# Quantised rows transposed in bfloat16 instead of float32, in a fused attention and integer-FFN kernel

## The chip, the cores and the metric

The kernel runs on one core of one Trainium2 chip. The metric is the device time of one execution in microseconds (us). A core has five engines that run side by side and wait for each other by semaphores: TensorE (PE in the profile; PEld is its weight load), VectorE (DVE), ScalarE (ACT), GpSimd (POOL) and SyncE (SP, which here only issues DMAs and waits). TensorE reads SBUF and writes PSUM banks; the other engines copy results out of the banks.

## The reference

`x` is (8, 512, 256) in f32. For each of 8 batches it is scaled by a style and normalised, goes through an attention with 16 heads of 16 columns whose projections are demodulated, gets a skip term, and then an FFN quantised to 8 bits whose result is added to `x`:

```python
x = x * s1[:, None, :];  x = (x - mu) * rsqrt(var + EPS_IN)
q = heads(einsum('bsh,oh->bso', x, q_weight) * q_dc);  k = ...;  v = ... * v_dc * s2
out = softmax(q k^T * scale) v
y = (out @ w_weight.T) * w_dc + (v_flat @ u_weight.T) * u_dc
# FFN, 8-bit integers:
lhs_scale = maximum(max(abs(y), axis=2), 1e-12) / 127
q_lhs = clip(round(y / lhs_scale), -127, 127)
q_rhs = clip(round(rhs / rhs_scale), -127, 127)
out = x + (q_lhs @ q_rhs) * lhs_scale * rhs_scale
```

## The kernel before

The program handles one batch per step, t = 0 to 7, in eight slots of a step (`for i in range(SUPER)`). A slot has two rounds of attention: `scores_of` (L1000), ScalarE's exponentials (L524) and `values_of` (L1014), and between them TensorE does "fill" work, listed by `step_fills` and issued by `fill` (L1211): projections for the next batch a = t+1, and the output and the FFN for the batches behind, z = t-1 and y = t-2. The order on each engine is written out by hand; `step_fills` also numbers the uses of a ring of three PSUM banks (`work`), which TensorE claims (`claim`, a wait on `work_freed`) and VectorE frees.

The FFN of batch z, in two halves i of 256 rows each: `output` (L1139) multiplies the attention result by the output weights; `quantise` on VectorE (L741) adds the skip term, takes each row's largest magnitude, forms the scale and its inverse, and makes integers in f32 that have the number MAGIC = 1.5 x 2^23 added, which rounds them; `quantised_transposed` (L1163) transposes them on TensorE by the f32 identity, all through the helper at L977; `integers` (L762) copies them out of the bank and takes MAGIC off again, with a bf16 result (`y_qt`), since whole numbers up to 127 are exact in bf16; `int_product` (L1179) multiplies them by the quantised right side in bf16. In a middle step the two transposes of batch z stand in slot 7 (before `output(z, 1)` and the norms) and slot 8 (behind the values of the next batch, the last work before the flag). The tile `y_q` is a view of the tile `o_t2`; the profile calls both `o_t`.

At the end of a step a flag is computed on VectorE (`bound_flag`, L687): whether the scores of the next batch are small enough to do without a shift by the row maximum. TensorE (`row_maxima`), SyncE (`load_shift`) and VectorE each load it into a register and branch on it; `scores_of` then waits until SyncE has said that the shift is done with.

The last batch has no further attention to hide behind; its two halves go through other banks and ScalarE.

At the start VectorE makes `head_ones` from the identity (L813), clears `q_stack` (L815), copies the transposed conditions (L817) and takes the statistics of the first batch; GpSimd meanwhile fills `k_stack` (L354) and `v_aug` (L357). The root of the variance is GpSimd's (L363), the normalisation VectorE's (L626).

Of the kernel before, what the change touches and what calls it, by code (L numbers as in the profile page):

```python
# [7 lines left out]
BF16 = mybir.dt.bfloat16  # L8
I32 = mybir.dt.int32
ALU = mybir.AluOpType  # L10
# [3 lines left out]
P = 128  # L14
INT8_MAX = 127.0
MAGIC = 1.5 * 2.0 ** 23
# [48 lines left out]
def adaln_ffn_kernel(nc, x, cond, wq, wk, wv, ww, wu, rhs, out):  # L65
    B, S, H = x.shape
    NH, D = 16, H // 16
    KT = S // P
    HC = H // P
# [34 lines left out]
    with ctx:  # L104
        def sb(name, shape, dt=F32):
            return ctx.enter_context(nc.sbuf_tensor(name, shape, dt))

        def sem(name):
            return ctx.enter_context(nc.semaphore(name))

        ident = sb("ident", [P, P])
# [59 lines left out]
        y_q = o_t2[:, :, :, :].rearrange("p i c t -> p (i c t)").rearrange("p (k o) -> p k o", k=KT)  # L171
# [4 lines left out]
        y_inv = sb("y_inv", [P, KT])  # L176
        demod_rows = o_nat[:, :, :].rearrange("p k h -> p (k h)")[0:B, 0:3 * H].rearrange(
            "b (m o) -> b m o", m=3)
        y_qt = sb("y_qt", [P, HC, S], BF16)


        by_two = [o_t2[:, :, :, :].rearrange("p m c t -> p (m c t)").rearrange("p (m c i) -> p m c i", m=2, c=HC),
# [30 lines left out]
        work_ready, work_freed = sem("work_ready"), sem("work_freed")  # L213
# [9 lines left out]
        on_ready, ot_ready, yq_ready, yqt_ready = sem("on_ready"), sem("ot_ready"), sem("yq_ready"), sem("yqt_ready")  # L223
# [359 lines left out]
        def _(dve):  # L583
            chain, taken = Tally(), Tally()

            def link(instruction):

                instruction.then_inc(dve_step, 1)
                chain.count += 1
                dve.wait_ge(dve_step, chain.count)  # L590

            def ready(*key):

                use = USE[key]
                assert use == taken.count, key
                taken.count += 1
                dve.wait_ge(work_ready, use + 1)
                return work[:, use % NW, :]
# [142 lines left out]
            def quantise(z, i):  # L741
                two = slice(2 * i, 2 * i + 2)
                y, scale = y_q[:, two, :], y_scale[:, z % 2, two]
                if z == B - 1:
                    dve.wait_ge(product_t, i + 1)
                    bank = work[:, USE[("y", z, i)] % NW, :]
                else:
                    bank = ready("y", z, i)
                link(nc.vector.tensor_tensor(y, bank.rearrange("p (k o) -> p k o", k=2), skip[:, z % 2, two, :], ALU.add))  # L749
                if z < B - 1:  # L750
                    dve.sem_inc(work_freed, 1)
                link(nc.vector.tensor_reduce(amax[:, two], y, AX.X, ALU.max, apply_absolute_value=True))  # L752
                link(nc.vector.tensor_scalar(scale, amax[:, two], EPS_AMAX, 1.0 / INT8_MAX, ALU.max, ALU.mult))
                link(nc.vector.reciprocal(y_inv[:, two], scale))
                for k in range(2):
                    last = nc.vector.tensor_scalar(y_q[:, 2 * i + k, :], y[:, k, :], y_inv[:, 2 * i + k:2 * i + k + 1],  # L756
                                                   -INT8_MAX, ALU.mult, ALU.max)
                link(last)
                nc.vector.tensor_scalar(y_q[:, two, :], y_q[:, two, :], INT8_MAX, MAGIC, ALU.min, ALU.add
                                        ).then_inc(yq_ready, 1)  # L760

            def integers(z, i):  # L762
                link(nc.vector.tensor_scalar(y_qt[:, :, 2 * i * P:2 * (i + 1) * P],
                                             ready("yqt", z, i).rearrange("p (c t) -> p c t", c=HC), MAGIC, None,
                                             ALU.subtract))
                dve.sem_inc(yqt_ready, 1)
                dve.sem_inc(work_freed, 1)

# [43 lines left out]
            with nc.allow_low_precision("sums of zeros and one 1"):  # L812
                link(nc.vector.tensor_reduce(head_ones[:, 0:HG].rearrange("p (e r) -> p e r", e=2),  # L813
                                             ident[:, :].rearrange("p (e d r) -> p e r d", e=2, d=D), AX.X, ALU.add))
            nc.vector.memset(q_stack[:, 0, :, :].bitcast(F32), 0.0).then_inc(q_cleared[0], 1)  # L815

            link(nc.vector.tensor_copy(cond_t[:, :, :], ready("cond", 0, 0)[:, 0:2 * HC * B].rearrange(  # L817
# [47 lines left out]
            for c in range(HC):  # L865
                bank = ready("xt", 0, c)
# [108 lines left out]
        def _(pe):  # L975
# [3 lines left out]
            def claim(*key):  # L979

                use = USE[key]
                if use >= NW:
                    pe.wait_ge(work_freed, use - NW + 1)
                return work[:, use % NW, :]
# [135 lines left out]
            def transpose_pair(bank, src, i, done):  # L1120

                for c in range(HC):
                    for k in range(2):
                        last = transpose(bank[:, (2 * c + k) * P:(2 * c + k + 1) * P],
                                         src[:, 2 * i + k, c * P:(c + 1) * P])
                last.then_inc(done, 1)
# [36 lines left out]
            def quantised_transposed(z, i):  # L1163
                pe.wait_ge(yq_ready, z * 2 + (i + 1))
                if z == B - 1:
                    transpose_pair(scores[:, 2 + i, :], y_q, i, integers_t)
                else:
                    transpose_pair(claim("yqt", z, i), y_q, i, work_ready)

            def int_product(z, i):  # L1170
                pe.wait_ge(yqt_ready, z * 2 + (i + 1))
# [245 lines left out]
```

## Time and profile before

| | us |
|---|---|
| median of three runs | 459.09 |
| the three runs | 459.18, 459.09, 457.11 |
| the profiled execution | 456.99 |
| its span in the profile | 455.2 |
| TensorE busy | 422.0 (93%) |
| ScalarE busy | 294.4 (65%) |
| VectorE busy | 243.1 (53%) |
| GpSimd busy | 108.2 (24%) |

Busy shares are taken over the whole span. TensorE's products overlap, and their ends in the profile are modelled, so the start-to-start distance of two groups tells what a group costs. "Idle before" in a row is the time in which the engine stood just ahead of that instruction, with the one that released it.

### The profile page before, as it was taken

The numbers are of one execution on the slowest core, as the hardware profiler recorded it, in microseconds if no ns is written. First come the engines' busy times: TensorE is split into PE (matmuls) and PEld (weight loads), VectorE is DVE, ScalarE is ACT, GpSimd is POOL, SyncE is SP. The second block draws the span as 40 slices with busy tenths as digits, with TensorE's granted clock in tenths as the row PEclk, the third lists the DMA queues.
The fourth block names the chain that finished last, engine by engine and source line by source line (L and its number), as shares of the span: only waits on it lengthen the run. The fifth ranks groups of instructions, "written<-read, shape, count | busy, mean of one in ns | idle before, by whom it ended". The sixth has DMA issues, their size and how long they took to land.

```text
span 455.2 us, 7727 instructions
## 1 busy us (share of the span) xinstructions
PE 422.0 (93%) x2684; PEld 233.9 (51%) x2684; DVE 243.1 (53%) x562; ACT 294.4 (65%) x343; POOL 108.2 (24%) x114
## 2 busy tenths in 40 slices
PE   8976499999999999999999999999999999999974
PEld 7744154455554555555545555455545555554444
DVE  6661346454466546745675447654675445436325
ACT  3523278767776686668765786667676776677741
POOL 7292212301111023301250024302340123002111
PEclk9797799999999999999999999999999999999999
DMA  5299239903991189215991299217961299102021
GB/s 174 85 131 155 30 120 137 117 8 111 135 125 55 35 175 147 67 50 149 132 137 54 92 142 139 93 36 151 136 102 55 68 132 159 49 1 94 0 94 46
DMA packets 29470, 44.59 MB, mean 98 GB/s; under 512 B 3896, under 2 KB 15160, under 8 KB 29400
## 3 DMA queue, kind: packets, MB, share of 16 engines
q1 hardware_dynamic: 27184, 38.71, 49.6%
q0 software_dynamic: 1040, 3.70, 2.5%
q10 hardware_dynamic: 1200, 1.59, 2.2%
q8 instruction: 26, 0.43, 0.5%
q14 instruction: 20, 0.16, 0.2%
HBM read 14.57 MB, written 4.25 MB: 41 GB/s over the span
## 4 chain that ended last, share of the span: by engine, by line
PE 81%; DVE 9%; DMA 5%; issue 3%; ACT 2%; DVEq 0%; POOL 0%; POOLq 0%
PE o_acc L1014 23%; PE scores L1000 16%; PE work L1065 10%; PE work L1042 9%; PE work L977 8%; PE work L1139 5%; DMA rows<-rows_dram 3%; PE work L1053 3%; DMA rows_dram<-o_nat 2%; PE work L1179 2%; DVE o_t L756 1%; PE work L1298 1%; DVE amax L752 1%; DVE o_t L749 1%; PE scores L1042 1%
## 5 line engine op out<-in xcount | busy, mean ns | idle before, releaser
L524 ACT ACTIVATE probs<-scores 128x1024 f32<-128x1024 f32 x256 | 247.8, 1024 | 111.2 <-PE scores L1000 111.2
L1014 PE MATMUL o_acc<-probs,v_aug 128*32 128x512 f32 x1024 | 124.4, 602 | 6.8 <-DVE skip L665 6.5
L1000 PE MATMUL scores<-q_stack,k_stack 50*128 50x512 f32 x512 | 96.6, 452 | 9.4 <-DMA k_stack<-parts 4.2
L402 POOL TENSOR_TENSOR squares<-parts 128x512 bf16<-128x512 f32 x32 | 33.5, 1048 | 208.2 <-ACT parts L508 208.2
L1000 PEld LDWEIGHTS scores<-q_stack,k_stack 50*128 50x128 f32 x512 | 39.6, 187 | 82.8 <-ACT probs L524 57.9
L1014 PEld LDWEIGHTS o_acc<-probs,v_aug 128*32 128x32 f32 x1024 | 26.6, 109 | 68.5 <-issue 56.0
L1065 PE MATMUL work<-vs_w,x_t 128*128 128x512 f32 x192 | 53.2, 420 | 0.9 <-DVEq L891 0.9
L1042 PE MATMUL work<-x_t,qk_w 128*128 128x512 f32 x168 | 44.5, 406 | 0.2 <-DVEq L634 0.2
L663 DVE TENSOR_TENSOR v_aug<-work,rows 128x256 f32<-128x256 f32 x32 | 13.6, 424 | 57.8 <-PE work L1065 44.5
L1065 PEld LDWEIGHTS work<-vs_w,x_t 128*128 128x128 f32 x192 | 35.9, 197 | 14.3 <-issue 6.2
L410 POOL TENSOR_TENSOR res<-res,x_res 128x512 f32<-128x512 f32 x15 | 19.1, 1275 | 73.9 <-DVEq L785 73.9
L1042 PEld LDWEIGHTS work<-x_t,qk_w 128*128 128x128 f32 x168 | 30.0, 188 | 7.1 <-issue 0.7
L977 PE MATMUL work<-ident,o_t 128*128 128x128 f32 x180 | 26.5, 276 | 0.0
L1139 PE MATMUL work<-w_demod,o_t 128*128 128x256 f32 x112 | 26.5, 379 | 0.0
L977 PEld LDWEIGHTS work<-ident,o_t 128*128 128x128 f32 x180 | 20.7, 140 | 6.4 <-issue 4.0
L532 ACT ACTIVATE o_t<-o_acc 128x512 f32<-128x512 f32 x32 | 19.2, 599 | 6.1 <-PE o_acc L1014 5.9
L1139 PEld LDWEIGHTS work<-w_demod,o_t 128*128 128x128 f32 x112 | 20.6, 190 | 2.7
L779 DVE SCALAR_TENSOR_TENSOR res<-work,y_scale,rhs_scale_row 128x256 f32<-128x256 f32 x28 | 12.3, 479 | 15.3 <-PE work L1179 15.0
L645 DVE SCALAR_TENSOR_TENSOR parts<-work,cols,parts 128x512 fp32r<-128x512 f32 x14 | 10.5, 750 | 17.7 <-ACT parts L508 17.7
L737 DVE COPY o_t<-work 128x512 f32<-128x512 f32 x14 | 9.7, 692 | 18.6 <-PE work L977 18.2
L626 DVE TENSOR_SCALAR x_sb<-x_sb,mv,rstd 128x256 f32<-128x256 f32 x32 | 11.3, 416 | 11.0 <-issue 11.0
L749 DVE TENSOR_TENSOR o_t<-work,skip 128x512 f32<-128x512 f32 x16 | 11.1, 692 | 11.0 <-PE work L1139 8.5
(149 smaller groups left out, 416.5 us busy)
## 6 DMA issues: line engine op xcount, KB each, us to landing
q_stack<-parts SPq DMA_DIRECT2D x96, 128.0 KB, 6.0
k_stack<-parts SPq DMA_DIRECT2D x88, 128.0 KB, 7.6
x_res<-in_x_dram SPq DMA_DIRECT2D x8, 512.0 KB, 4.3
x_sb<-in_x_dram SPq DMA_DIRECT2D x7, 512.0 KB, 3.6
out_dram<-res POOLq DMA_DIRECT2D x7, 512.0 KB, 6.9
rows<-rows_dram SPq DMA_DIRECT2D x8, 384.0 KB, 3.3
rows<-in_cond_dram SPq DMA_DIRECT2D x8, 128.0 KB, 3.6
k_stack<-parts ACTq DMA_DIRECT2D x8, 128.0 KB, 9.9
```

What stands on the lines that cost most here:

```text
L402: nc.gpsimd.tensor_tensor(squares[:, n, :], parts[:, n, 0, :], parts[:, n, 0, :], ALU.mult).then_inc(squares_ready, 1)
L410: nc.gpsimd.tensor_tensor(res[:, two, :], res[:, two, :], x_res[:, two, :], ALU.add).then_inc(res_added, 1)
L524: nc.scalar.activation(probs[:, r % RING, pair:pair + 2, :], scores[:, pair:pair + 2, :], ACT.Exp).then_inc(exp_done, 1)
L532: nc.scalar.activation(o_t[:, group % G, :], o_acc[:, :], ACT.Copy).then_inc(o_saved, 1)
L749: link(nc.vector.tensor_tensor(y, bank.rearrange("p (k o) -> p k o", k=2), skip[:, z % 2, two, :], ALU.add))
L977: return nc.tensor.transpose(dst, src, ident[0:rows, 0:rows])
L1000: last = nc.tensor.matmul(scores[:, 2 * (u % 2) + e, :], k_stack[top:top + ROWS, t % 2, 2 * g + u % 2, kt * P:(kt + 1) * P], q_stack[top:t ...
L1014: last = nc.tensor.matmul(o_acc[DV * j:DV * (j + 1), :], v_aug[:, kt, 4 * g + j, :], probs[:, r % RING, j, :], start=(kt == 0), stop=(kt = ...
L1042: last = nc.tensor.matmul(bank, lhs, right, start=(n == 0), stop=(n == len(operands) - 1))
L1053: last = nc.tensor.matmul(bank[:, hc * H:(hc + 1) * H], wv_scaled[:, c, hc * P:(hc + 1) * P], wu_t[:, c, :], start=(c == 0), stop=(c == HC ...
L1065: last = nc.tensor.matmul(bank, lhs, right, start=(n == 0), stop=(n == len(operands) - 1))
L1139: last = nc.tensor.matmul(bank[:, k * H:(k + 1) * H], o_t2[:, i, c, k * P:(k + 1) * P], w_demod[:, z % 2, c, :], start=(c == 0), stop=(c = ...
```

## The change

For batches 0 to 6, `quantise` multiplies by the inverse scale and adds MAGIC in the first operation (before: multiply and lower bound), still f32 and in place, and then takes MAGIC off and applies the upper bound 127 in the second, with a bf16 result in a new tile `y_int`. TensorE transposes `y_int` by an ordinary product with a bf16 identity, `ident_b`, in place of the f32 transposes. `integers` applies the lower bound -127 in the copy out of the bank, where it took MAGIC off before. `ident_b` is cast once from the f32 identity, on VectorE at the start, with a wait on its result behind it. The last batch is as before.

```diff
--- before.py
+++ after.py
@@ -177,6 +177,8 @@
         demod_rows = o_nat[:, :, :].rearrange("p k h -> p (k h)")[0:B, 0:3 * H].rearrange(
             "b (m o) -> b m o", m=3)
         y_qt = sb("y_qt", [P, HC, S], BF16)
+        y_int = sb("y_int", [P, KT, H], BF16)
+        ident_b = sb("ident_b", [P, P], BF16)
 
 
         by_two = [o_t2[:, :, :, :].rearrange("p m c t -> p (m c t)").rearrange("p (m c i) -> p m c i", m=2, c=HC),
@@ -752,6 +754,15 @@
                 link(nc.vector.tensor_reduce(amax[:, two], y, AX.X, ALU.max, apply_absolute_value=True))
                 link(nc.vector.tensor_scalar(scale, amax[:, two], EPS_AMAX, 1.0 / INT8_MAX, ALU.max, ALU.mult))
                 link(nc.vector.reciprocal(y_inv[:, two], scale))
+                if z < B - 1:
+                    for k in range(2):
+                        last = nc.vector.tensor_scalar(y_q[:, 2 * i + k, :], y[:, k, :], y_inv[:, 2 * i + k:2 * i + k + 1],
+                                                       MAGIC, ALU.mult, ALU.add)
+                    link(last)
+
+                    nc.vector.tensor_scalar(y_int[:, two, :], y, MAGIC, INT8_MAX, ALU.subtract, ALU.min
+                                            ).then_inc(yq_ready, 1)
+                    return
                 for k in range(2):
                     last = nc.vector.tensor_scalar(y_q[:, 2 * i + k, :], y[:, k, :], y_inv[:, 2 * i + k:2 * i + k + 1],
                                                    -INT8_MAX, ALU.mult, ALU.max)
@@ -761,8 +772,8 @@
 
             def integers(z, i):
                 link(nc.vector.tensor_scalar(y_qt[:, :, 2 * i * P:2 * (i + 1) * P],
-                                             ready("yqt", z, i).rearrange("p (c t) -> p c t", c=HC), MAGIC, None,
-                                             ALU.subtract))
+                                             ready("yqt", z, i).rearrange("p (c t) -> p c t", c=HC), -INT8_MAX, None,
+                                             ALU.max))
                 dve.sem_inc(yqt_ready, 1)
                 dve.sem_inc(work_freed, 1)
 
@@ -812,6 +823,7 @@
             with nc.allow_low_precision("sums of zeros and one 1"):
                 link(nc.vector.tensor_reduce(head_ones[:, 0:HG].rearrange("p (e r) -> p e r", e=2),
                                              ident[:, :].rearrange("p (e d r) -> p e r d", e=2, d=D), AX.X, ALU.add))
+                link(nc.vector.tensor_copy(ident_b[:, :], ident[:, :]))
             nc.vector.memset(q_stack[:, 0, :, :].bitcast(F32), 0.0).then_inc(q_cleared[0], 1)
 
             link(nc.vector.tensor_copy(cond_t[:, :, :], ready("cond", 0, 0)[:, 0:2 * HC * B].rearrange(
@@ -1165,7 +1177,14 @@
                 if z == B - 1:
                     transpose_pair(scores[:, 2 + i, :], y_q, i, integers_t)
                 else:
-                    transpose_pair(claim("yqt", z, i), y_q, i, work_ready)
+
+                    bank = claim("yqt", z, i)
+                    for c in range(HC):
+                        for k in range(2):
+                            last = nc.tensor.matmul(bank[:, (2 * c + k) * P:(2 * c + k + 1) * P],
+                                                    y_int[:, 2 * i + k, c * P:(c + 1) * P], ident_b[:, :],
+                                                    start=True, stop=True)
+                    last.then_inc(work_ready, 1)
 
             def int_product(z, i):
                 pe.wait_ge(yqt_ready, z * 2 + (i + 1))
```

The changed kernel has other line numbers, so rows are matched by operation and names. VectorE at the start of the program, before (L815 clears `q_stack`, L841 scales the first batch by its style):

```order
L810 MEMSET head_ones 128x16
L813 TENSOR_REDUCE head_ones<-ident 128x8
L815 MEMSET q_stack 128x4096
L817 COPY cond_t<-work 128x32
L820 TENSOR_TENSOR cond_sq<-cond_t 128x32
L841 TENSOR_TENSOR x_sb<-x_sb,rows 128x512
```

and of the change:

```order
L821 MEMSET head_ones 128x16
L824 TENSOR_REDUCE head_ones<-ident 128x8
L826 CAST ident_b<-ident 128x128
L827 MEMSET q_stack 128x4096
L829 COPY cond_t<-work 128x32
L832 TENSOR_TENSOR cond_sq<-cond_t 128x32
L853 TENSOR_TENSOR x_sb<-x_sb,rows 128x512
```

The cast of the identity stands between the reduction and the memset; the rest follows in the same order.

TensorE from slot 7 of a middle step to the flag, before (`o_t` in the first row is the quantised tile; L1139 is `output`, L1073 the norms, L1065 the values of the next batch, and the last row of transposes holds both `to_natural` and the quantised rows):

```order
L977 MATMUL work<-ident,o_t 128x128 x4
L1139 MATMUL work<-w_demod,o_t 128x256 x4
L1073 MATMUL work<-squares,head_ones 32x512 x4
L1000 MATMUL scores<-q_stack,k_stack 128x512 x4
L1014 MATMUL o_acc<-probs,v_aug 32x512 x8
L1000 MATMUL scores<-q_stack,k_stack 128x512 x4
L977 MATMUL work<-ident,norm_max 1x128
L1065 MATMUL work<-vs_w,x_t 128x512 x6
L977 MATMUL work<-ident,o_t 128x128 x8
```

and of the change (L1184 is the new product, L1151 the `output` that was L1139):

```order
L1184 MATMUL work<-ident_b,y_int 128x128 x4
L1151 MATMUL work<-w_demod,o_t 128x256 x4
L1085 MATMUL work<-squares,head_ones 32x512 x4
L1012 MATMUL scores<-q_stack,k_stack 128x512 x4
L1026 MATMUL o_acc<-probs,v_aug 32x512 x8
L1012 MATMUL scores<-q_stack,k_stack 128x512 x4
L989 MATMUL work<-ident,norm_max 1x128
L1077 MATMUL work<-vs_w,x_t 128x512 x6
L989 MATMUL work<-ident,o_t 128x128 x4
L1184 MATMUL work<-ident_b,y_int 128x128 x4
```

The two groups of four stand where they stood; only their kind changes.

VectorE in the same slot, `quantise` and the norms behind it, before:

```order
L749 TENSOR_TENSOR o_t<-work,skip 128x512
L752 TENSOR_REDUCE amax<-o_t 128x2
L753 TENSOR_SCALAR y_scale<-amax 128x2
L754 RECIPROCAL y_inv<-y_scale 128x2
L756 TENSOR_SCALAR o_t<-o_t,y_inv 128x256 x2
L759 TENSOR_SCALAR o_t<-o_t 128x512
L673 TENSOR_REDUCE norm_max<-work 128x1
```

and of the change:

```order
L751 TENSOR_TENSOR o_t<-work,skip 128x512
L754 TENSOR_REDUCE amax<-o_t 128x2
L755 TENSOR_SCALAR y_scale<-amax 128x2
L756 RECIPROCAL y_inv<-y_scale 128x2
L759 TENSOR_SCALAR o_t<-o_t,y_inv 128x256 x2
L763 TENSOR_SCALAR y_int<-o_t 128x512
L675 TENSOR_REDUCE norm_max<-work 128x1
```

The number of operations and their shapes stay; the last of `quantise` writes `y_int`.

## Rows read from the trace of the kernel before

**Rows 1.** the page, its busy shares (part 1) and the chain that ended last (part 4).

```profile
PE 422.0 (93%) x2684; PEld 233.9 (51%) x2684; DVE 243.1 (53%) x562; ACT 294.4 (65%) x343; POOL 108.2 (24%) x114
...
PE 81%; DVE 9%; DMA 5%; issue 3%; ACT 2%; DVEq 0%; POOL 0%; POOLq 0%
```

**Rows 2.** timeline: start us, us, engine, operation, [idle before <-releaser]; slot 7 of a middle step.

```profile
232.83 0.66 PE L977 MATMUL work<-ident,o_t 128*128 128x128 f32 x4
...
233.32 1.89 PE L1139 MATMUL work<-w_demod,o_t 128*128 128x256 f32 x8
...
235.25 0.69 DVE L749 TENSOR_TENSOR o_t<-work,skip 128x512 f32<-128x512 f32 x1 [1.04 <-PE work L1139]
...
236.71 1.88 POOL L389 TENSOR_SCALAR wv_scaled<-wv_nat,cols 128x256 f32<-128x256 f32 x2
...
238.31 0.55 DVE L759 TENSOR_SCALAR o_t<-o_t 128x512 f32<-128x512 f32 x1
...
239.51 0.27 PE L977 MATMUL work<-ident,norm_max 128*1 128x128 f32 x1 [0.79 <-DVE norm_max L673]
```

**Rows 3.** timeline of a middle step's end.

```profile
390.58 0.14 DVE L687 TENSOR_SCALAR flag<-bound 1x1 int32<-1x1 f32 x1
...
390.67 1.03 PE L977 MATMUL work<-ident,o_t 128*128 128x128 f32 x8
...
392.46 0.73 PE L1000 MATMUL scores<-q_stack,k_stack 50*128 50x512 f32 x4 [0.76 <-SPq L273]
```

**Rows 4.** timeline: two products of the integers, then transposes.

```profile
226.94 0.61 PE L1179 MATMUL work<-rhs_q,y_qt 128*128 128x256 bf16 x4
...
227.39 0.60 PE L977 MATMUL work<-ident,o_t 128*128 128x128 f32 x4
```

**Rows 5.** timeline of the last step, TensorE.

```profile
419.26 1.09 PE L977 MATMUL work<-ident,o_t 128*128 128x128 f32 x8
...
421.21 0.50 PE L1000 MATMUL scores<-q_stack,k_stack 50*128 50x512 f32 x2 [0.42 <-ACT probs L524]
...
426.03 0.50 PE L1000 MATMUL scores<-q_stack,k_stack 50*128 50x512 f32 x2 [0.34 <-ACT probs L524]
```

**Rows 6.** single lines of VectorE: duration ns min/median/max.

```profile
L763 DVE TENSOR_SCALAR y_qt<-work x14: 683/692/692, 133.7 to 424.9; 128x512 bf16<-128x512 f32 x14
...
L759 DVE TENSOR_SCALAR o_t<-o_t x16: 426/428/554, 127.0 to 447.8; 128x512 f32<-128x512 f32 x16
```

**Rows 7.** the same view, line L621.

```profile
L621 DVE TENSOR_SCALAR var_eps<-mv x7: 170/170/347, 35.5 to 333.5; 128x4 f32<-128x4 f32 x7
```

**Rows 8.** timeline of the program's start, VectorE, GpSimd and TensorE.

```profile
1.78 0.38 DVE L813 TENSOR_REDUCE head_ones<-ident 128x8 bf16<-128x128 f32 x1 [0.90 <-POOL ones L352]
...
2.07 3.51 POOL L354 MEMSET k_stack<- 128x4096 f32 x1
...
3.08 3.47 DVE L815 MEMSET q_stack<- 128x4096 f32 x1 [0.92 <-DVE head_ones L813]
...
6.19 1.83 POOL L357 MEMSET v_aug<- 128x2048 f32 x1
...
10.49 1.05 POOL L363 TENSOR_TENSOR rstd<-var_eps,half 128x4 f32<-128x4 f32 x1 [2.46 <-DVE var_eps L849]
...
12.50 1.37 DVE L626 TENSOR_SCALAR x_sb<-x_sb,mv,rstd 128x256 f32<-128x256 f32 x4
...
18.07 5.47 PE L1042 MATMUL scores<-x_t,qk_w 128*128 128x512 f32 x12
```

**Rows 9.** timeline: a later GpSimd memset and L621 beside it.

```profile
32.28 3.51 POOL L425 MEMSET q_stack<- 128x4096 f32 x1
...
35.47 0.35 DVE L621 TENSOR_SCALAR var_eps<-mv 128x4 f32<-128x4 f32 x1
```

**Rows 10.** the chain in order of time: start us, us, what.

```profile
34.17 14.54 DMA rows<-rows_dram
```

**Rows 11.** a stretch: us, busy (x) of PE, PEld, DVE, ACT, POOL, PEclk, DMA, GB/s.

```profile
16.80:23.60 6.80, 6.80 (x22) 5.35 (x22) 2.66 (x5) 3.30 (x7) 3.25 (x8) 0.50 0.31 104
```

## The prediction

> **What bounds the kernel now.** I read the page's busy shares first, then the chain of waits, then the timeline of one middle step, of the last step and of the first 50 us, and last the groups of instructions by shape. TensorE is busy for 93% of the span and carries 81% of the chain that ended last; VectorE has 9% of it [rows 1]. A middle step (one batch of attention, in eight slots) is a TensorE stream with two places where it stands. In the seventh slot TensorE waits for a VectorE chain: the product L1139 ends, VectorE adds, reduces and quantises (L749 to L759), then takes the largest norms (L673), and only then can TensorE transpose the norms: 0.79 us idle at 239.51 [rows 2]. At the step's end TensorE waits until the flag has been read: in the 390 us step the eight transposes start at 390.67 and end at 391.70, the scores start at 392.46, released by SyncE (L273), while the flag was written at 390.58 + 0.14 = 390.72 [rows 3]. The scores come 1.74 us behind the flag, and the transposes end 0.76 us earlier than that.
>
> **TensorE: what is removed.** Each batch but the last has two groups of four f32 transposes of the quantised rows; the change makes each a group of four bf16 products, 14 groups in all. A group costs from 232.83 to the start of L1139 at 233.32, 0.49 us [rows 2]. No row shows a bf16 product with 128 columns. The nearest is L1179, bf16 with 256 columns: four take from 226.94 to 227.39, 0.11 us each [rows 4]. Halving the columns gives at best 0.055 us each; if the weight loads set the pace it stays 0.11. The last one still has to cover the load of f32 weights for L1139, for which I leave 0.11. I take 3 x 0.055 + 0.11 = 0.28 us for a group, a gain of 0.21 us; the ends are a gain of 0.05 (pace 0.11 throughout, 0.44) and of 0.27 (0.22 in all). A group slower than 0.49 I exclude: L1179 moves twice the columns in 0.45.
> The Trainium skill, "TensorE: Matmul & The Clock Gate", section "Back-to-back issue gap", gives about 81 ns for each pair of a weight load and a 128-column product in a stream; by it a group would be 0.32 us or a little more and the gain up to 0.17, an estimate from that page, which no row here shows.
>
> **Which groups lie on the path.** The first group of a batch (slot 7) stands before L1139, whose end releases VectorE's add after an idle VectorE [rows 2], and everything up to the norms, the values, the flag and the next scores hangs on that. So its 0.21 us passes through, in six middle steps: 6 x 0.21 = 1.26 us. The second group (slot 8) is the later half of the eight transposes at 390.67. It ends before the flag has been read, so a faster group only lengthens the idle time: gain 0 in six steps, as long as the scores wait for the flag [rows 3]. Of the last two groups, in the last step, the first is in the eight at 419.26; the scores behind it wait for ScalarE's exponentials (0.42 us idle at 421.21), and the second group stands before such a wait too (0.34 us idle at 426.03) [rows 5]. Gain 0. TensorE in all: -1.3 us, not 14 x 0.21 = 2.9.
>
> **VectorE in the steps.** The two operations with the scale (L756) keep form and shape. The third, L759, 128x512 f32 in place in 426 to 554 ns, now writes bf16. The one bf16 write of that size that VectorE does in the steps takes 692 ns, but it reads from a bank (L763); L759 reads from SBUF [rows 6]. I take no change; the upper end is 692 ns. On the path lies only the one in slot 7, which took 0.55 us beside GpSimd's L389 [rows 2]: at 0.69 it would cost 6 x 0.14 = 0.8 us. The lower end, were half the bytes quicker, is some 0.1 us each, 0.6 in all. The copy out of the bank (L763) keeps its size and its one operation: 0.
>
> **VectorE at the start: what is added.** One cast of the identity, 128x128 f32 to bf16, goes between the reduction L813 and the memset of q_stack L815, with a wait behind it. Alone it is cheap: between L621's 170 ns (4 elements [rows 7]) and L759's 426 (512), so about 0.23 us, plus 0.15 for the wait. Behind it on VectorE are the memset, the copy of the conditions (L817), the modulation and statistics of the first batch; GpSimd's root (L363) waits for them, and VectorE's L626 for the root. The root is done at 10.49 + 1.05 = 11.54 and L626 starts at 12.50, so there is 0.96 us of cover [rows 8]. Alone the cast is hidden.
> But GpSimd starts its memset of k_stack at 2.07 and holds it until 5.58 [rows 8], while L813 ends at 2.16. The trace has one like pair: L621, VectorE's tensor-scalar in SBUF, began at 35.47 while GpSimd's memset L425 ran to 35.79. It took 347 ns against 170 in its other runs, and ended at 35.82, just behind the memset [rows 7, 9]. Against it: L759 beside GpSimd's tensor-scalar L389 lost 0.12 us, though L389 stood on GpSimd from 236.71 to 238.59 [rows 2]. So the bounds are 0 (hidden) and a cast held until 5.58, or even until the second memset ends at 6.19 + 1.83 = 8.02 [rows 8]. By the row nearest in kind, L621, I take the first memset. The cast then ends near 5.73, 3.57 us after L813. The q_stack memset ended 4.39 us after L813 (6.55 against 2.16), so it ends near 10.1, and L817, the statistics and the root come 3.6 us later. After the cover of 0.96, L626 is 2.6 to 2.7 us late. On it hang the transposes, the first projections (18.07), the store of the row scales and the load of rows, which lands at 34.17 + 14.54 = 48.7 and for which the first values wait [rows 10]. Nothing on that way is idle for another reason, so I take +2.7. The granted clock from 16.8 to 23.6 is 0.50, the 1.2 GHz level [rows 11]; how much of the projections falls into such a stretch can move this by about 0.5 either way.
> The Trainium skill, "SBUF — State Buffer", section "Who interferes with whom", says that GpSimd and a VectorE copy, cast or tensor-scalar between SBUF tiles that uses both port pairs exclude each other for a whole instruction. By that rule the cast waits for the memset; L621's 347 ns agrees with it, L759 beside L389 only in part; a cast held to 5.58 is what the sum already has.
>
> **The sum.** The profiled execution took 456.99 us, span 455.2 plus 1.8 around it. -1.3 (TensorE) + 0 (quantising) + 2.7 (start) = +1.4: 458.4 for such an execution. The three runs have a median of 459.09 and the profiled one lies below all of them; the four average 458.1. I apply the +1.4 to that mean, 459.5.
>
> **Rivals.**
> 1. The cast is not held: it fits between GpSimd's writes, as L759 nearly does beside L389. Only -1.3 remains: 456.8. For it: a memset reads nothing. Against: L621.
> 2. The cast is held by both memsets (slower). The second, L357, starts at 6.19, with a GpSimd DMA issue between them; if VectorE gets no turn there, the cast ends near 8.2, 6.0 us after L813, and L626 is 5.1 late: 5.1 - 1.3 = +3.8, 461.9. It decides once the cast ends after about 6.7, where the loss passes 2.3 us. Against: 0.6 us lie between the memsets.
> 3. The change doesn't do what it says on TensorE: bf16 products with 128 columns run at the pace of L1179, 0.11 us, and gain 0.05 a group, or the bf16 write costs 0.14 a step. With the cast held: 2.7 - 0.3 + 0.8 at most, +2.4 to +3.2, about 461.
> 4. All 14 groups count and the cast is hidden: -2.9, 455.2. Against: the idle 0.76 behind the flag and the waits for ScalarE.
>
> **How the numbers follow.** Forecast (cast held once, first groups gained) 0.48, rival 1 0.24, rival 2 0.09, rival 3 0.12, rival 4 0.07. Half a per cent is 2.3 us, about what a measurement of this kernel tells from no change. Faster by more: rival 4 and a little of rival 1, 0.10. Slower by more: rivals 2 and 3 and a tail of the forecast, 0.27. Within: 0.63. The range, 456.3 to 462.2, holds rivals 1 and 2; below it lies rival 4. The forecast's own range is 458.0 to 461.0, since both signs hold much of the chance.
>
> **What would show it.** In the profile after: the cast's start and end against GpSimd's k_stack memset, the end of the q_stack memset near 10, L626 near 15.2, the rows landing near 51.4. In a middle step: L1139 starting 0.28 us behind the first bf16 product, the VectorE chain behind it as long as before, and an idle time before the scores of the next step that is about 0.2 us longer than 0.76. A cast that takes 0.2 us makes the forecast wrong by 2.7 us; a step shorter by 0.4 us would mean that both groups count.

## The result, and the profile after

| | before | after |
|---|---|---|
| median of 6 runs each, on one chip, us | 458.68 | 461.14 |
| lowest to highest | 457.11 to 459.18 | 460.93 to 464.02 |
| ratio of the two | | 1.0067, 95% interval 1.0044 to 1.0089 |
| profiled execution | 456.99 | 461.23 |
| its span | 455.2 | 459.4 |
| VectorE busy | 243.1 | 249.0 |

The change makes the kernel slower by 0.4 to 0.9%, some 2.0 to 4.1 us. That lies in the predicted range (456.3 to 462.2), but the range had been drawn to hold rivals 1 and 2 as well, so lying in it says little of the mechanism; the change is nearer the number of rival 2 (+3.8) than that of the forecast (+1.4).

The page of the changed kernel, busy shares:

```profile
PE 422.4 (92%) x2684; PEld 234.1 (51%) x2684; DVE 249.0 (54%) x563; ACT 294.3 (64%) x343; POOL 108.0 (24%) x114
```

VectorE has one instruction more and 5.9 us more of busy time against [rows 1]. The timeline of the changed kernel's start shows which instruction that is, beside [rows 8]:

```profile
2.07 3.51 POOL L356 MEMSET k_stack<- 128x4096 f32 x1
2.19 5.91 DVE L826 CAST ident_b<-ident 128x128 bf16<-128x128 f32 x1
5.53 0.67 POOL L358 DMA_DIRECT2D zero_dram<-probs  x1
6.19 1.83 POOL L359 MEMSET v_aug<- 128x2048 f32 x1
9.03 3.47 DVE L827 MEMSET q_stack<- 128x4096 f32 x1 [0.92 <-DVE ident_b L826]
...
17.52 1.38 DVE L628 TENSOR_SCALAR x_sb<-x_sb,mv,rstd 128x256 f32<-128x256 f32 x4 [0.21 <-POOL rstd L365]
```

The cast is on VectorE from 2.19 to 8.10. GpSimd's first memset ends at 5.58, its second at 8.02; the cast ends 0.08 behind the second. The q_stack memset ends at 12.50 (before: 6.55), and the normalisation starts at 17.52 instead of 12.50, now straight behind the root. From there the delay travels down the chain in order of time, which answers to [rows 10]:

```profile
31.35 8.10 DMA rows_dram<-o_nat
39.47 13.89 DMA rows<-rows_dram
```

The rows land at 53.36, against 48.71 before: 4.65 us late, and the first values with them.

A middle step of the changed kernel, TensorE's timeline (with two rows of VectorE between), answers to [rows 2, 3]:

```profile
237.20 0.40 PE L1184 MATMUL work<-ident_b,y_int 128*128 128x128 bf16 x4
237.44 1.95 PE L1151 MATMUL work<-w_demod,o_t 128*128 128x256 f32 x8
...
242.47 0.55 DVE L763 TENSOR_SCALAR y_int<-o_t 128x512 bf16<-128x512 f32 x1
...
243.67 0.27 PE L989 MATMUL work<-ident,norm_max 128*1 128x128 f32 x1 [0.77 <-DVE norm_max L675]
...
244.79 0.14 DVE L689 TENSOR_SCALAR flag<-bound 1x1 int32<-1x1 f32 x1
...
245.24 0.60 PE L989 MATMUL work<-ident,o_t 128*128 128x128 f32 x4
245.67 0.39 PE L1184 MATMUL work<-ident_b,y_int 128*128 128x128 bf16 x4
246.76 0.73 PE L1012 MATMUL scores<-q_stack,k_stack 50*128 50x512 f32 x4 [0.71 <-issue]
```

The group in slot 7 holds L1151 back by 0.24 us (237.20 to 237.44), where the f32 group took 0.49. The quantising, now into bf16, takes the same 0.55 us beside GpSimd, and the wait for the norms the same 0.77. The second group ends at 246.05, and TensorE then stands 0.71 us until the scores.

The length of the six middle steps can be read from the first and the last of the flags. The view of the tile `flag` between 85 and 400 us; columns: duration ns min/median/max, first to last start in us. Before:

```profile
L687 DVE TENSOR_SCALAR flag<-bound x7: 141/141/142, 91.7 to 390.6; 1x1 int32<-1x1 f32 x7
```

After:

```profile
L689 DVE TENSOR_SCALAR flag<-bound x7: 141/141/143, 96.3 to 394.0; 1x1 int32<-1x1 f32 x7
```

By the timeline's two decimals (91.66, 390.58; 96.35, 393.96) the six steps take 298.92 us before and 297.61 after: -1.31. Not all of it is the transposes: the first five steps are 0.74 shorter (0.15 each), the sixth 0.57. In the sixth, VectorE of the kernel before paused on the flag's chain. Its timeline there, before:

```profile
390.19 0.17 DVE L681 TENSOR_TENSOR norm_prod<-norm_row 1x16 f32<-1x16 f32 x1 [0.52 <-DVE norm_row L678]
```

and after:

```profile
393.57 0.16 DVE L683 TENSOR_TENSOR norm_prod<-norm_row 1x16 f32<-1x16 f32 x1
```

The copy ahead of it started at 389.39 and at 393.15: 0.80 us from one to the other before, 0.42 after. Of the ten kernels below three have the pause at the last flag (the two that double transposes, and the one whose cast is on ScalarE) and seven have not, among them the one that is the kernel before with a cast; so it does not go with the kind of transposes. So I read 0.93 us as the transposes' own and 0.38 as this pause's. The kernel before with the cast has no such pause; its six steps (flags at 97.50 and 396.14) take 298.64 us, 1.03 more than the changed kernel's, which bears this out within 0.1.

So +4.65 at the start and -1.31 in the steps, +3.3. The profiled executions differ by 4.2 us; the remaining 0.9 is mostly behind the last flag, in the tail, where the granted clock fell in this execution. A stretch of the changed kernel (us, busy of the engines, then PEclk, DMA, GB/s), and the two rows of the timeline of the same products, after:

```profile
444.90:448.40 3.50, 3.50 (x10) 2.75 (x10) 1.57 (x4) 0.00 (x0) 0.00 (x0) 0.53 0.00 0
...
444.68 3.68 PE L1165 MATMUL work<-w_demod,o_t 128*128 128x256 f32 x8 [0.47 <-ACT o_t L576]
```

and before:

```profile
441.31 1.99 PE L1153 MATMUL work<-w_demod,o_t 128*128 128x256 f32 x8 [0.47 <-ACT o_t L574]
```

Eight products took 3.68 us at a granted clock of 0.53, almost all of it the 1.2 GHz level, where they took 1.99 at the upper one; of these 1.69 us only 0.8 reach the end, by the distance from the last flag to the end of the span (64.6 us before, 65.4 after). Of the ten other kernels below two show it too (3.3 and 3.4 us for these eight products) and eight do not (2.0), so I count it to no part of the change.

### The profile page after: what moved, and what is told of

The parts are those of the page before. It is cut to its first block, busy times and chain, and to the rows that moved or that the text cites. A ratio compares the mean times of both kernels' runs of the same rounds, so it can differ in the third digit from the quotient of the medians.

```text
span 459.4 us, 7728 instructions
## 1 busy us (share of the span) xinstructions
PE 422.4 (92%) x2684; PEld 234.1 (51%) x2684; DVE 249.0 (54%) x563; ACT 294.3 (64%) x343; POOL 108.0 (24%) x114
## 4 chain that ended last, share of the span: by engine, by line
PE 79%; DVE 11%; DMA 5%; issue 3%; ACT 1%; POOL 0%; DVEq 0%; POOLq 0%
PE o_acc L1026 23%; PE scores L1012 16%; PE work L1077 10%; PE work L1054 9%; PE work L989 7%; PE work L1151 5%; DMA rows<-rows_dram 3%; PE work L1065 3%; DMA rows_dram<-o_nat 2%; PE work L1198 2%; DVE ident_b L826 1%; PE work L1165 1%; PE scores L1054 1%; ACT probs L526 1%; DVE o_t L759 1%
## 5 line engine op out<-in xcount | busy, mean ns | idle before, releaser
L1151 PE MATMUL work<-w_demod,o_t 128*128 128x256 f32 x112 | 26.8, 382 | 0.0
L1151 PEld LDWEIGHTS work<-w_demod,o_t 128*128 128x128 f32 x112 | 20.6, 190 | 2.7
L989 PE MATMUL work<-ident,o_t 128*128 128x128 f32 x124 | 18.8, 274 | 0.0
L365 POOL TENSOR_TENSOR rstd<-var_eps,half 128x4 f32<-128x4 f32 x8 | 8.3, 1041 | 35.7 <-DVE var_eps L623 27.2
```

What stands on the lines that cost most here:

```text
L989: return nc.tensor.transpose(dst, src, ident[0:rows, 0:rows])
L1151: last = nc.tensor.matmul(bank[:, k * H:(k + 1) * H], o_t2[:, i, c, k * P:(k + 1) * P], w_demod[:, z % 2, c, :], start=(c == 0), stop=(c = ...
```

## The experiments

Ratios are to the kernel before, with 95% intervals; its median in the three sets was 457.99, 457.92 and 458.62 us.

**The cast alone, in the kernel before.**

```diff
+        ident_b = sb("ident_b", [P, P], BF16)
...
+                link(nc.vector.tensor_copy(ident_b[:, :], ident[:, :]))
```

> The kernel before plus the cast of the identity alone, at the place where the change has it; its result is used by nothing. Theory 1 (the loss is all in the start, because GpSimd's memsets hold the cast): the cast takes 5.9 us again, ends near 8.1, the first values' products behind the load of rows start 4.6 to 4.8 us later than in the kernel before (49.62 to about 54.3), the middle steps keep 49.9 to 50.1 us, and the time is 4 to 5 us above the kernel before, some 1.5 us above the change itself. Rival (the loss comes from the bf16 products or the new tile in the steps): the cast is as short as 0.2 to 0.4 us here, or the time is within 1 us of before.

Measured: 463.57 us, ratio 1.0111 (1.0073 to 1.0148), +3.3 to +6.8 us. The timeline of VectorE's start and the chain:

```profile
2.19 5.91 DVE L816 CAST ident_b<-ident 128x128 bf16<-128x128 f32 x1
```

```profile
40.47 13.30 DMA rows<-rows_dram
```

The cast takes the same 5.91 us, the normalisation starts at 17.51, and the rows land at 53.77. By the middle of the ratios this one unused instruction costs more (+5.1 us) than the whole change (+3.1), whose other parts give something back; the two intervals overlap.

**The cast on ScalarE.** It stands behind the instruction with ScalarE's first table load; the rest is the change.

```diff
-                link(nc.vector.tensor_copy(ident_b[:, :], ident[:, :]))
...
+            nc.scalar.activation(ident_b[:, :], ident[:, :], ACT.Copy)
```

> The change with the identity cast by ScalarE behind its table load, in place of VectorE. Theory 1: VectorE's q_stack memset starts near 3.1 as in the kernel before, nothing at the start is late, and only TensorE's gain is left: 1.2 to 1.5 us faster than before, ratio about 0.997, middle steps 0.15 to 0.25 us shorter. Rival (the bf16 group costs elsewhere what it gains): no faster than before within 0.3 us.

Measured: 457.60 us, ratio 0.9985 (0.9961 to 1.0009). The timeline:

```profile
3.07 3.47 DVE L827 MEMSET q_stack<- 128x4096 f32 x1 [0.92 <-DVE head_ones L825]
3.75 0.29 ACT L460 ACTIVATE ident_b<-ident 128x128 bf16<-128x128 f32 x1
...
11.72 1.37 DVE L629 TENSOR_SCALAR x_sb<-x_sb,mv,rstd 128x256 f32<-128x256 f32 x4
...
15.44 5.13 PE L1346 MATMUL work<-cond_sq,probs 128*128 128x8 f32 x24
```

ScalarE casts in 0.29 us under the same memset, and the delay of VectorE at the start is gone. Whether the 1.3 us of the steps arrive, the ratio can't tell: its interval runs from -1.8 to +0.4 us. The profiled execution took 459.58 us, where the twelve of this kernel go from 456.52 to 459.96, and it shows what can eat a gain: the granted clock was at the lower level from 11.6 to 25.3, the 24 small products took 5.13 us (3.36 before), and the rows landed at 51.02 although the normalisation began 0.8 us earlier than in [rows 8]. Stretches of this kernel:

```profile
11.60:25.30 13.70, 12.98 (x51) 11.54 (x50) 6.69 (x18) 6.25 (x12) 2.60 (x8) 0.50 0.22 73
```

**A product in place of the cast.** Same engine, same place; the identity times itself is the identity.

```diff
-                link(nc.vector.tensor_copy(ident_b[:, :], ident[:, :]))
+                link(nc.vector.tensor_tensor(ident_b[:, :], ident[:, :], ident[:, :], ALU.mult))
```

> The change with the cast replaced, at the same place on VectorE, by a product of the identity with itself (two inputs in SBUF, same shapes and types, same wait behind it). Theory 1a (only the kinds copy, cast and tensor-scalar, which run at two elements a cycle between SBUF tiles, wait for GpSimd's memset): it runs at once, 0.2 to 0.4 us long, and the time is 1 to 1.5 us under before. Theory 1b (any VectorE read or write of SBUF waits behind a memset of GpSimd that started earlier): it takes 5.9 us like the cast and the time is 2.5 to 4 us over before. Rival (the extra instruction and its wait are slow for a reason of their own, such as fetching): also long, but not ending at GpSimd's 8.02.

Measured: 456.28 us, ratio 0.9948 (0.9926 to 0.9971). The timeline's start, beside the same k_stack memset (2.07 to 5.58):

```profile
2.20 0.29 DVE L826 TENSOR_TENSOR ident_b<-ident 128x128 bf16<-128x128 f32 x1
3.41 3.47 DVE L827 MEMSET q_stack<- 128x4096 f32 x1 [0.92 <-DVE ident_b L826]
```

The normalisation starts at 12.27. The same bytes in and out took 0.29 us instead of 5.91. So it is neither the size, the conversion nor the place that is slow, but the kind of instruction beside GpSimd's write. The Trainium skill, "SBUF — State Buffer", section "Who interferes with whom", tells the two apart: a cast can take both port pairs and then excludes GpSimd, while an operation with two SBUF inputs collides only with a GpSimd instruction that reads. By that rule the product passes a memset; the trace agrees, 0.29 against 5.91 us.

**The second memset out of the way.** `v_aug` is filled behind the first root instead of before it.

```diff
-            nc.gpsimd.memset(v_aug[:, :, :, :], 1.0).then_inc(pool_setup, 1)
...
             inverse_root(0)
+            nc.gpsimd.memset(v_aug[:, :, :, :], 1.0).then_inc(pool_setup, 1)
```

> The change with GpSimd's second memset (v_aug, 1.83 us) moved behind the first root, so that GpSimd stands idle after the issue of its DMA at about 6.2. Theory 1 (the cast gets its turn only when GpSimd has nothing going on): the cast ends at 6.2 to 6.4, 1.8 us earlier than in the change, and the time is 1.5 to 2 us under the change. Rival A (it gets its turn as soon as the first memset ends, and what held it in the change was something else): the cast ends near 5.6 to 5.8. Rival B (GpSimd has no part in it): the cast still ends near 8.1.

Measured: 462.71 us, ratio 1.0088 (1.0063 to 1.0114). The timeline:

```profile
2.19 3.47 DVE L826 CAST ident_b<-ident 128x128 bf16<-128x128 f32 x1
...
14.92 1.79 POOL L419 MEMSET v_aug<- 128x2048 f32 x1
14.99 2.84 DVE L628 TENSOR_SCALAR x_sb<-x_sb,mv,rstd 128x256 f32<-128x256 f32 x4
```

With nothing behind the first memset the cast ends at 5.66, 0.1 behind it. I had expected 6.2 to 6.4, the end of GpSimd's DMA issue; 5.66 is the end that rival A names, though not its cause, as the next two kernels show. The time did not improve, which I had not expected either: the moved memset now ran beside the four normalisations, which took 2.84 us instead of 1.38. The first of them alone was held (1.88 us, against a median of 0.41 for this line; the second starts at 16.79, and the memset ends at 16.71), the other three took their usual 1.04 together: again a hold to the end of a memset. The lower clock came on top (granted 0.50 while the 24 products took 5.13 us).

**GpSimd waits for the cast.**

```diff
+            pool.wait_ge(dve_step, 3)
             nc.gpsimd.memset(v_aug[:, :, :, :], 1.0).then_inc(pool_setup, 1)
```

> The change, with one wait added: GpSimd starts its second memset (v_aug) only when the cast of the identity is done. Theory (the cast is held by whatever memset GpSimd runs or has taken up without a turn for VectorE between them, and the first alone ends at 5.6): the cast ends between 5.6 and 5.9, v_aug's memset runs from about 5.8 to 7.7, the q_stack memset ends near 10.1, L628 starts near 14.8 against 17.5 in the change; the rows land near 51.3 and the time is some 2.4 us below the change, about +0.2 % above the kernel before. Rival (the cast takes 5.9 us for a reason of its own, or waits for a fixed time): it ends at 8.1 still, the v_aug memset comes after it, and the time is that of the change, 461. Second rival: the cast gets no turn because GpSimd's DMA issue holds too; then it ends only after the issue, near 6.2, and L628 comes near 15.3.

Measured: 460.45 us, ratio 1.0052 (1.0027 to 1.0076). The timeline and the chain:

```profile
2.19 3.47 DVE L827 CAST ident_b<-ident 128x128 bf16<-128x128 f32 x1
6.19 1.83 POOL L360 MEMSET v_aug<- 128x2048 f32 x1
...
15.07 1.38 DVE L629 TENSOR_SCALAR x_sb<-x_sb,mv,rstd 128x256 f32<-128x256 f32 x4 [0.21 <-POOL rstd L366]
...
17.44 4.94 PE L1347 MATMUL work<-cond_sq,probs 128*128 128x8 f32 x24
```

```profile
38.32 14.06 DMA rows<-rows_dram
```

This is the forecast's own case: cast done at 5.66, normalisation 2.57 us late (forecast 2.6 to 2.7). The second memset starts at 6.19 as in the change, so the wait cost GpSimd nothing, and the DMA issue between the memsets (5.53 to 6.20) held nothing up: the second rival falls. But the rows land at 52.38, 3.67 late and not 2.6: the 24 products took 4.94 us at a granted clock of 0.52, against 3.36 at 0.79 before. 3.67 - 1.31 = 2.36 us, and the ratio says +2.4 (1.2 to 3.5).

**GpSimd waits for its own first memset.**

```diff
+            pool.wait_ge(k_cleared, 1)
             nc.gpsimd.memset(v_aug[:, :, :, :], 1.0).then_inc(pool_setup, 1)
```

> The change, with one wait added: GpSimd starts its second memset (v_aug) only when its own first one (k_stack) has written its last value; nothing waits for VectorE. Theory A (in the change the second memset is taken up while the first still runs, so that the claim passes from one to the other and VectorE gets no turn): the wait opens a turn, the cast ends at 5.66 as in the version that waits for the cast, and L628 starts near 15.1. Theory B (only a GpSimd that waits for the cast itself leaves VectorE a turn; between two memsets it never gets one): the cast ends at 8.1 and L628 starts at 17.5, as in the change.

Measured: 461.18 us, ratio 1.0044 (1.0022 to 1.0065). The timeline and the chain:

```profile
2.19 3.46 DVE L827 CAST ident_b<-ident 128x128 bf16<-128x128 f32 x1
...
6.18 1.83 POOL L360 MEMSET v_aug<- 128x2048 f32 x1
...
18.26 5.13 PE L1347 MATMUL work<-cond_sq,probs 128*128 128x8 f32 x24
```

```profile
40.42 13.30 DMA rows<-rows_dram
```

Theory A holds as far as it tells the two apart: a wait that has nothing to do with VectorE opens the turn. In all three kernels the second memset's record begins at 6.18 or 6.19, so its start doesn't show the difference; only whether GpSimd had to wait for its own write first does. That the claim is passed on while the first memset still runs is my reading of it; the trace shows only that it goes away with the wait.

The whole time doesn't show the turn. The normalisation starts at 15.06, as with the wait for the cast, but the rows land at 53.72, later even than the change's 53.36: from 16 to 20 us the granted clock was 0.50 here (0.74 in the change), and the 24 products took 5.13 us instead of 3.63. The ratios of the three kernels, +3.1 us (2.0 to 4.1), +2.4 (1.2 to 3.5) and +2.0 (1.0 to 3.0), overlap. So it is shown that the wait brings the cast and the normalisation 2.45 us forward, and not shown that it makes the kernel faster.

**The transposes of one half done twice, in the kernel before**, slot 7 or slot 8, batches 0 to 5. Shown for slot 7; for slot 8 the condition is i == 1.

```diff
+                    bank = claim("yqt", z, i)
+                    if i == 0 and z < B - 2:
+                        for c in range(HC):
+                            for k in range(2):
+                                transpose(bank[:, (2 * c + k) * P:(2 * c + k + 1) * P],
+                                          y_q[:, 2 * i + k, c * P:(c + 1) * P])
+                    transpose_pair(bank, y_q, i, work_ready)
```

> The kernel before, with the four f32 transposes of the first half (slot 7) done twice into the same bank for batches 0 to 5; nothing else differs. Four more cost 0.43 us at their pace of 0.108. Theory (slot 7 lies on the path): each of the six steps is 0.43 longer, +2.6 us in all (+0.56 %). Rival (hidden, as VectorE or ScalarE sets the slot): no change.

> The kernel before, with the four f32 transposes of the second half (slot 8) done twice into the same bank for batches 0 to 5. Theory (the idle time ahead of the flag's scores, 0.43 to 0.76 us, covers them): the idle time before the scores falls by 0.43 to 0.0 to 0.3 and the time stays within 0.1 %; where VectorE's copy of the bank (0.69 us, behind the transposes) is late for the row shift ahead of the scores, up to 0.4 a step. Rival (both groups count alike): +2.6 us, as in slot 7.

Measured: slot 7 461.44 us, ratio 1.0070 (1.0046 to 1.0093); slot 8 459.59 us, ratio 1.0015 (0.9992 to 1.0038). The flags, slot 7:

```profile
L687 DVE TENSOR_SCALAR flag<-bound x7: 141/141/143, 93.2 to 395.0; 1x1 int32<-1x1 f32 x7
```

and slot 8, with the scores behind a flag:

```profile
L687 DVE TENSOR_SCALAR flag<-bound x7: 141/141/142, 91.9 to 391.0; 1x1 int32<-1x1 f32 x7
...
241.49 1.47 PE L977 MATMUL work<-ident,o_t 128*128 128x128 f32 x12
...
242.89 0.73 PE L1000 MATMUL scores<-q_stack,k_stack 50*128 50x512 f32 x4
```

Six steps take 301.83 us (93.19 to 395.02), +2.91, with four more transposes in slot 7, and 299.09 (91.88 to 390.97), +0.17, with four more in slot 8, where the scores now start as the transposes end. The same work costs 2.91 us in one slot and 0.17 in the next.

**Only the first half in bf16**, with the product in place of the cast:

```diff
-                if z < B - 1:
+                if z < B - 1 and i == 0:
...
+                elif i == 1:
+                    transpose_pair(claim("yqt", z, i), y_q, i, work_ready)
```

> The change with the cast as a product of the identity with itself, and with the second half (slot 8) as in the kernel before: f32 integers with MAGIC added, f32 transposes, MAGIC taken off in the copy. Only the first half (slot 7) is bf16. Theory (the whole gain of TensorE is that of the first halves, the second ones only lengthen the wait for the flag): the last six steps sum to 297.6 as with both halves, the idle time before the scores of the flag is 0.4 instead of 0.7, and the time is that of the version with both (456.3, -0.5 %). Rival (both halves count): the last six steps sum to 298.3, 0.65 more.

Measured: 456.06 us, ratio 0.9945 (0.9919 to 0.9970). The flags, and the scores behind a flag:

```profile
L689 DVE TENSOR_SCALAR flag<-bound x7: 141/141/143, 91.4 to 389.0; 1x1 int32<-1x1 f32 x7
...
241.88 0.73 PE L1013 MATMUL scores<-q_stack,k_stack 50*128 50x512 f32 x4 [0.48 <-issue]
```

Six steps: 297.57 us (91.39 to 388.96), against 297.6 with both halves. The second half's bf16 is worth nothing here; it only turns 0.48 us of idle time into 0.7.

**Filling the wait for the flag**, with the product in place of the cast. In TensorE's order (VectorE's follows):

```diff
                 if i == 0:
-                    values(t, 1)
+                    if first:
+                        values(t, 1)
                     values(t, 2)
+                    if y >= 0:
+                        quantised_transposed(y, 1)
...
                         values(a, 0)
+                        values(a, 1)
                         to_natural(t, 2)
...
-                        else:
-                            quantised_transposed(z, 1)
```

> The change, with two differences. The cast of the identity is a product of the identity with itself (two inputs, on VectorE, same place), which GpSimd's memset did not hold. And the work around the flag is put in another order: the second quarter of the next batch's values (v_and_skip and its six products, 1 to 1.3 us of TensorE) moves from the next step's slot 1 to slot 8, before the wait for the flag, and the second half's transposes of the integers from slot 8 to slot 1 of the next step. Theory (TensorE stands 0.7 us idle at the flag in each of seven steps, so work brought before it is free): up to 0.7 us a step, -3 to -5 us against the version without the new order (456.3), 452 to 453. Rival (VectorE's copy of the quarter, 0.7 us, now stands before the row shift and the flag's chain ends later by as much; or the exponentials of slot 1 set the pace there): no gain, 456 or up to 2 us more.

Measured: 451.82 us, ratio 0.9863 (0.9837 to 0.9889), the fastest of all. TensorE at the end of the step, and the flags:

```profile
238.05 3.04 PE L1080 MATMUL work<-vs_w,x_t 128*128 128x512 f32 x12
...
239.07 0.14 DVE L690 TENSOR_SCALAR flag<-bound 1x1 int32<-1x1 f32 x1
...
240.93 0.60 PE L992 MATMUL work<-ident,o_t 128*128 128x128 f32 x4
...
241.46 0.73 PE L1015 MATMUL scores<-q_stack,k_stack 50*128 50x512 f32 x4
```

```profile
L690 DVE TENSOR_SCALAR flag<-bound x7: 141/142/142, 92.0 to 386.0; 1x1 int32<-1x1 f32 x7
```

Twelve products instead of six stand between the norms and the transposes, and the scores (241.46) start as the last transposes end (241.53): the idle time is gone. Six steps take 294.08 us (91.97 to 386.05), 3.5 less than the 297.6 of the old order.

## Why the prediction was right and wrong

**The start: the mechanism was right, the memset was not.** The forecast held the cast until 5.58, the end of GpSimd's first memset; it was held until the second one's end at 8.02. The failed step is "by the row nearest in kind, L621, I take the first memset", and with it the sentence against rival 2, that 0.6 us lie between the memsets. GpSimd had nothing ready behind L621's memset: its next instruction, the root at 35.90, needs L621's own result. So that row could not tell about two memsets in a row. I mis-sized the delay of the normalisation by 2.4 us: 2.57 with one memset (the kernel in which GpSimd waits for the cast), 5.02 with two. Rival 2 had foreseen 5.1 and 461.9; it deserved far more than 0.09, since the only thing against it was a gap in which GpSimd's own next instruction was ready too.

**From VectorE to the rows: the way right, the margin for the clock too small.** The 5.02 us on VectorE arrived as 4.65 with the rows. The forecast left 0.5 us either way for the clock. In the change that was enough, but by luck: with one memset 2.57 became 3.67 in one kernel and 2.56 became 5.01 in the next (GpSimd waiting for its own memset), and with the cast on ScalarE, where the normalisation came 0.78 early, the rows came 2.31 late. In those three the 24 products took 4.94 to 5.13 us, in the change 3.63 and before 3.36.

**TensorE in the steps: the mechanism right, the size nearly.** The group was to cost 0.28 us instead of 0.49. L1151 starts 0.24 behind the first product, but its own first product then takes 0.05 longer than before, so the group brings 0.20 (forecast 0.21). Of the forecast's 6 x 0.21 = 1.26 us, 0.93 arrived: about 0.05 a step was lost again between the flag and the scores (1.92 us before and 1.97 after in the step at 240 us), a place where I had assumed nothing would change. The second group's kind is not the cause, since it is 1.96 with that group in f32; the cause stays open. That the flags give 1.31, close to the forecast's 1.26, is chance, by the pause of 0.38. That the second groups count nothing is shown twice, by doubling them (+0.17 us, against +2.91 in slot 7) and by leaving them in f32 (no difference). The idle time before the scores was to grow by 0.2 us; in the step at 240 us it grew from 0.43 to 0.71.

**Quantising: right.** L763 writes bf16 in 426 to 554 ns, as L759 wrote f32 [rows 6]; the copy out of the bank, 0.69 us, too. Rival 3 falls on both counts.

**Rivals 1 and 4** fall with the cast. What spoke for rival 1, L759 beside L389 [rows 2], decides nothing: L389 is no memset, and L759 ends at 238.86, 0.27 us behind L389's end at 238.59, so the row is open to a hold as well. But the kernel with the product, in which nothing is held at the start, shows what they were worth: -2.4 us (-3.4 to -1.3), of which the steps are 1.31. Where the other 1 us comes from, if it is there, stays open: the start of that kernel was no earlier (its rows landed at 48.95 against 48.71), and the interval reaches down to 1.3.

**The sum.** +4.65 - 1.31 = +3.3 us; the ratio says +3.1 (2.0 to 4.1). The agreement is looser than it looks. The sum compares one execution of each kernel, and the kernel before was profiled at 456.99 us, where 28 executions of the first set go from 456.74 to 461.95, with a mean granted clock of about 0.973 in those near 457 and 0.965 in those near 459.5. What is firm is where the loss comes from: the cast alone brings it (+3.3 to +6.8 us), and the same change with a product in the cast's place has none of it (-2.4 us).

## What to carry to other kernels

Before a cheap VectorE copy, cast or tensor-scalar between SBUF tiles is put beside GpSimd's fills, see how many of them follow each other: here the cast outlasted two, and an operation with two inputs, or ScalarE, does the same thing in 0.29 us. Of two equal savings in one step, only that counts which has no wait of another engine behind it; where such a wait is idle time of the bound engine, work from behind it that needs nothing of what is waited for is worth more (3.5 us here) than making the work ahead of it faster (nothing).

## What the runs showed that was not expected

- A cast held by a GpSimd memset gets no turn at its end if the next memset is queued behind it without a wait on the first: 5.91 us instead of 3.47, although 0.6 us lie between the two records. A wait of GpSimd on its own first memset, which does not move the second's record (6.18), is enough to let it through.
- Later in the start of the changed kernel a single memset held `var_eps`, as it held L621 in [rows 9]: 0.77 us against a median of 0.17, ending at 41.00, just behind the memset's end at 40.97:

```profile
37.46 3.51 POOL L427 MEMSET q_stack<- 128x4096 f32 x1
...
40.23 0.77 DVE L623 TENSOR_SCALAR var_eps<-mv 128x4 f32<-128x4 f32 x1
```

- Four bf16 products with 128 columns, each with its weight load, run at about 0.06 us each (four in 0.24 us to the next group's start). The Trainium skill, "TensorE: Matmul & The Clock Gate", section "Back-to-back issue gap", gives 81 ns for a long stream of such pairs; this group of four was quicker, and no long stream is in this kernel.
- What a delay at the start costs depends on where the lower clock then falls: the same 24 small products took 2.74 us in one kernel (the cast alone in the kernel before, granted clock 1.00) and 5.13 in others (0.50), which is more than the bf16 transposes bring in all.
